# Attention values multiplied by half-height matmuls, and a ring of 20 slots: one change to an attention and ternary-FFN kernel

## The chip, the cores and the metric

The kernel runs on one NeuronCore of one Trainium2 chip. The metric is the device time of one execution in microseconds. TensorE is called PE here, its weight loads PEld, VectorE DVE, ScalarE ACT, GpSimd POOL, and SyncE's queue, which issues nearly all transfers, SP.

## What is computed

For each of 64 batches, x is 512 rows of 512, and the context 77 rows of 512:

```
q  = layernorm(x) @ Wq                    # 4 groups x 4 kv heads of 32; rope
k, v = ctx @ Wk, ctx @ Wv                 # 4 kv heads of 32; rope on k
score[h] = sum over groups g of q[g, h] @ k[h].T / sqrt(32)
x1 = x + mean over h of (softmax(score[h]) @ v[h]) @ Wo
xq = clip(round(layernorm(x1) / i_scale)) # i_scale = max |layernorm(x1)| / 127, over ALL batches
out = x1 + (xq @ ternary(W).T) * w_scale * i_scale + bias
```

Since the scores are summed over the groups, the kernel sums Wq over them beforehand and has 4 heads per row. Two things matter for this change: the product of the softmax with v, and that i_scale needs all of x1 before the first FFN product, so that the kernel has two stages.

## The kernel before

**Prologue.** The context is projected to keys and values, which are written to two scratch tensors in HBM (k_scr, v_scr), and the weights are prepared.

**Stage A** (steps 0 to 127 and a tail; `steps`, L295) works on half a batch per step: two tiles of 128 rows of x, called t = 0, 1. It is a software pipeline of eight stages (L81: PROJ, ROPE, SCORE, VALUE, HEAD, RESID, STAT, RSTD); step i does PROJ for half-batch i, ROPE for i-1, SCORE for i-2, VALUE for i-3 and so on. Each engine has its own instruction stream, in the order written; semaphores join them. PE's order in a step (L1183 to L1276): transposes of the rotated q (qr_sb) and of the head sums (os_sb), 16 transposes of x, 10 transposes of the exponentials (e_sb), scores (L1239), output projection y (L1250), projection of x (L1258), values (L1273). Transposes, scores and y use 64 of the 128 rows of the PE array each (HALF = 64), in pairs: one instruction with rows 0 to 63, one with rows 64 to 127. The projection and the values use all 128 rows.

The keys of the two tiles stand side by side in e_sb: 2 x 4 heads x 77 = 616 columns, cut in five chunks of 128 (`STARTS`, L51). A chunk's 128 columns become the rows of pT_sb; the values of the same keys stand in v_blk, each head's 34 columns (32 values, their mean with Wo, a one for the sum of the exponentials) in its own place with zeros elsewhere, so that heads don't mix. A chunk touches three heads (the middle one two), and all five accumulate in one PSUM bank:

```
for c in (0, 2, 4, 1, 3):
    at0, n = FIRST_HEAD[c] * VC, HEADS_OF[c]
    last = pe.matmul(bank[6][:, at0:at0 + n * VC], pT_sb[:, c, :], v_blk[:, slot, c, 0:n, :]..., start=c == 0, stop=c == 3)
last.then_inc(pv_done, 1)
```

ACT then copies the bank out (L698), and has in the same step, in this order, the copies of the transposed q (L709), of the transposed head sums (L717) and of the transposed x (L725).

**SP's queue in stage A** (L439 to L462), per batch and strictly in order: both halves of x of batch b (each after `added_t` says that the slot of batch b-4 is free), the store of x1 of batch b-4 to the output tensor, 12 small loads of values of batch b-1 (`v_fetch`, after `pv_done`), 4 small loads of keys of batch b (`k_fetch`, after `sc_done`). The last 16 batches' x1 stay in SBUF (SLOTS = KEPT = 16, x1_sb); 48 are stored and come back later. x itself has a ring of four batches (x_sb), and in stage B its place serves other tiles.

**Stage B** (L1292 to L1339 on PE) takes the batches from the slots: ACT and DVE quantise, PE transposes (L1300) and multiplies in fp16 with half-height pairs (L1317), ACT adds the mean, DVE the product (L1052), SP writes the result (`result_out`) and brings the next stored x1 in (`x1_back`). The two row halves of the PE array never add to one bank at the same time: each product is made in two parts, with the banks changed between them, and the wait `ffn_half` (L1307) in between; the next transposes stand between the parts.

## Time and profile before

| what | value |
|---|---|
| median of 3 runs | 1137.72 us (1136.8 to 1142.96) |
| the profiled execution | 1138.31 us, of which the span is 1136.5 us |
| PE busy | 1075.1 us, 95% of the span |
| DVE busy | 1015.8 us, 89% |
| ACT busy | 963.0 us, 85% |
| POOL busy | 729.6 us, 64% |
| stage A, about | 115 to 815 us of the span |
| stage B, about | 820 to 1136.5 us of the span |

The profile is of one execution. Its own time stands beside its span; the difference of 1.8 us lies around the span. Busy shares of the whole span mix two stages with different limits, so each stage has to be read by itself. A PE matmul's recorded length runs to the end of its result, and matmuls overlap, so the pace of a group is read from its starts.

### The profile page before, as it was taken

The page shows a single profiled execution, that of the slowest core. Times are in us where ns is not written, and L with a number is a line of the kernel's source. Part 1 is how long each engine was busy: PE and PEld are TensorE (multiplying, and loading weights), DVE is VectorE, ACT ScalarE, POOL GpSimd, SP SyncE. Part 2 cuts the span into 40 slices and gives each one's busy share as a digit, 9 for nine tenths or more (in the row PEclk, how much of TensorE's full clock was granted, in tenths as well). Part 3 has the DMA queues.
Part 4 walks back from the last instruction along what each step waited for, and adds up shares of the span by engine and source line. Part 5 has one row for each costly group of instructions (what it writes and reads, how often), then busy time and mean ns, then how long its engine had stood idle before and what let it go on. Part 6 is the DMA issues. An engine that isn't in the chain of part 4 may idle for free.

```text
span 1136.5 us, 44893 instructions
## 1 busy us (share of the span) xinstructions
PE 1075.1 (95%) x14007; PEld 865.5 (76%) x14007; DVE 1015.8 (89%) x1836; ACT 963.0 (85%) x2147; POOL 729.6 (64%) x1547
## 2 busy tenths in 40 slices
PE   7998999999999999999999999999599999999991
PEld 6997988988989988998889998998455555555540
DVE  4653898999999999999999999999789999999981
ACT  4564888988989889988899989999599999999980
POOL 4675998999999999999999999999500000000000
PEclk9999999999999999999999999999599999999996
DMA  8765366666676666766667653432049999999996
GB/s 290 228 176 162 85 205 189 211 189 214 177 223 183 210 216 187 221 194 198 207 195 222 184 154 106 121 104 67 1 180 408 421 424 426 426 407 371 411 395 267
DMA packets 119897, 262.97 MB, mean 231 GB/s; under 512 B 65193, under 2 KB 76649, under 8 KB 99378
## 3 DMA queue, kind: packets, MB, share of 16 engines
q1 hardware_dynamic: 119810, 262.44, 68.2%
q8 instruction: 17, 0.28, 0.1%
q14 instruction: 22, 0.18, 0.0%
q10 hardware_dynamic: 48, 0.07, 0.0%
HBM read 139.79 MB, written 122.64 MB: 231 GB/s over the span
## 4 chain that ended last, share of the span: by engine, by line
POOL 34%; issue 24%; PE 12%; ACT 9%; DMA 8%; DVE 6%; SPq 3%; POOLq 1%; ACTq 1%; DVEq 0%
POOL qa_sb L559 6%; POOL pw_sb L589 6%; POOL qr_sb L599 5%; ACT x_sb L789 5%; PE y_ps L1113 5%; DMA out_y<-x_sb 5%; POOL pw_sb L605 4%; POOL os_sb L619 3%; POOL o_sb L610 3%; DVE x_sb L1052 3%; ACT x_sb L772 2%; DMA x_sb<-out_y 2%; POOL ve_sb L576 2%; SPq L378 2%; POOL rs_sb L583 2%
## 5 line engine op out<-in xcount | busy, mean ns | idle before, releaser
L1258 PEld LDWEIGHTS xT_ps<-wqs,xT_sb 128*128 128x128 f32 x2048 | 239.2, 192 | 48.3 <-ACT xT_sb L725 48.3
L1258 PE MATMUL xT_ps<-wqs,xT_sb 128*128 128x128 f32 x2048 | 263.6, 282 | 2.8 <-ACT xT_sb L725 2.8
L978 DVE SCALAR_TENSOR_TENSOR x_sb<-x_sb,mv_sb,y_ps 128x512 f32 (+1 forms) x256 | 177.9, 736 | 3.2 <-PE y_ps L1250 3.2
L789 ACT ACTIVATE x_sb<-x_sb,mean 128x512 f32 (+1 forms) x256 | 168.7, 707 | 0.0
L1273 PE MATMUL pT_ps<-v_blk,pT_sb 128*128 128x102 f32 (+1 forms) x1280 | 163.6, 275 | 0.0
L689 ACT ACTIVATE sq_sb<-x_sb 128x512 bf16 (+1 forms) x256 | 160.8, 628 | 1.0 <-DVE x_sb L978 0.8
L1273 PEld LDWEIGHTS pT_ps<-v_blk,pT_sb 128*128 128x128 f32 x1280 | 155.2, 194 | 1.7 <-ACT pT_sb L738 1.0
L985 DVE TENSOR_REDUCE amax<-x_sb (+1 forms) x128 | 155.1, 1213 | 0.0
L748 ACT ACTIVATE e_sb<-e_sb,rs_sb 128x308 f32<-128x308 f32 x256 | 127.3, 544 | 16.2 <-DVE e_sb L961 6.6
L725 ACT ACTIVATE xT_sb<-xT_ps 128x1024 f32<-128x1024 f32 x128 | 131.3, 1026 | 3.0 <-PE xT_ps L1180 2.9
L1317 PE MATMUL sc_ps<-wT,x_sb 64*128 64x512 f16 x1024 | 133.5, 380 | 0.1
L583 POOL TENSOR_TENSOR rs_sb<-ve_sb,mhalf 128x4 f32 (+2 forms) x133 | 132.3, 995 | 0.5
L948 DVE TENSOR_REDUCE mx_sb<-sc_ps 128x8 f32<-128x616 f32 x128 | 102.4, 800 | 33.4 <-PE sc_ps L1239 28.8
L1317 PE MATMUL pT_ps<-wT,x_sb 64*128 64x512 f16 x1024 | 132.1, 377 | 0.1
L559 POOL TENSOR_TENSOR qa_sb<-q_sb,qcos 128x256 f32<-128x256 f32 x128 | 93.8, 733 | 28.4 <-ACT q_sb L756 22.2
L1239 PE MATMUL sc_ps<-k_blk,qT_sb 64*128 64x154 f32 x1024 | 101.5, 315 | 0.4 <-ACT oT_sb L717 0.3
L961 DVE TENSOR_TENSOR e_sb<-sc_ps,mx_sb 128x616 f32<-128x616 f32 x128 | 98.2, 767 | 0.0
L1250 PE MATMUL y_ps<-wst,oT_sb 64*128 64x512 f32 x512 | 96.9, 449 | 0.9 <-ACT oT_sb L717 0.9
L1052 DVE SCALAR_TENSOR_TENSOR x_sb<-sc_ps,cols,x_sb 128x512 f32 (+1 forms) x128 | 90.2, 747 | 7.8 <-PE sc_ps L1317 2.3
L698 ACT ACTIVATE pv_sb<-pT_ps 128x272 f32<-128x272 f32 x128 | 50.9, 398 | 53.2 <-PE pT_ps L1273 53.2
L772 ACT ACTIVATE x_sb<-x_sb,rs_sb 128x512 f32 (+1 forms) x128 | 85.4, 714 | 12.5 <-DMA x_sb<-out_y 5.6
L599 POOL TENSOR_TENSOR qr_sb<-qa_sb,qb_sb 128x256 f32<-128x256 f32 x128 | 93.7, 732 | 0.1
(140 smaller groups left out, 2286.0 us busy)
## 6 DMA issues: line engine op xcount, KB each, us to landing
out_y<-x_sb SPq DMA_DIRECT2D x112, 1024.0 KB, 10.2
x_sb<-in_x SPq DMA_DIRECT2D x128, 512.0 KB, 5.1
x_sb<-out_y SPq DMA_DIRECT2D x48, 1024.0 KB, 15.3
x_sb<-in_ctx SPq DMA_DIRECT2D x38, 256.0 KB, 4.5
k_blk<-k_scr SPq DMA_DIRECT2D x256, 9.6 KB, 1.7
v_blk<-v_scr SPq DMA_DIRECT2D x256, 10.2 KB
v_scr<-x_sb SPq DMA_DIRECT2D x38, 68.0 KB, 3.1
k_scr<-x_sb SPq DMA_DIRECT2D x38, 64.0 KB, 3.4
```

The lines of the kernel that those rows point to most:

```text
L559: pool.tensor_tensor(dst[:, :].rearrange("p (t h d) -> p t h d", t=2, h=HEADS), q_sb[:, :].rearrange("p (t h d) -> p t h d", t=2, h=HEADS) ...
L583: pool.tensor_tensor(rs_sb[:, bass.ds(js, 1), :, at].rearrange("p a t n -> p (a t) n"), ve_sb[:, k % 2, :, at], mhalf[:, :, at], ALU.pow). ...
L599: pool.tensor_tensor(qr_sb[:, kj % 2, :].rearrange("p (a b) -> p a b", b=2), qa_sb[:, :].rearrange("p (a b) -> p a b", b=2), swapped(qb_sb ...
L689: act.activation(sq_sb[:, :], x1_at(kj, gj, t), ACT.Square, scale=E ** -0.5, accum_out=mv_sb[:, (kj + BACK) % UN, t, 2:3]).then_inc(sq_don ...
L725: act.activation(xT_sb[:, :, :, :].rearrange("p t c (h r) -> p (t c) h r", h=2), rows_of(xT_ps, 0, 2 * EC), ACT.Copy).then_inc(xT_copied, 1)
L748: act.activation(e_sb[:, kj % 2, t, :], e_sb[:, kj % 2, t, :], ACT.Exp, scale=rs_sb[:, bass.ds(j, 1), t, 0]).then_inc(exp_done_t, 1)
L789: act.activation(u_sb[:, k % 2, t, :], x1_sb[:, bass.ds(x1_turn(g, k) + t * E, E)], ACT.Identity, bias=stat_of(mean1, j, t, back)).then_in ...
L978: dve.scalar_tensor_tensor(out=x1_at(kj, gj, t), in0=x_sb[:, kj // 2, 2 * (kj % 2) + t, :], scalar=mv_sb[:, kj, t, 0:1], in1=y_ps[:, t, :] ...
L985: dve.tensor_reduce(amax[:, bass.ds(2 * j, 2)], x1_at(kj, gj).rearrange("p (t e) -> p t e", t=2), AX.X, ALU.max, apply_absolute_value=True ...
L1258: last = pe.matmul(bank[0][:, t * HD:(t + 1) * HD], xT_sb[:, t, c, :], wqs[:, c, :], start=c == 0, stop=c == EC - 1)
L1273: last = pe.matmul(bank[6][:, at0:at0 + n * VC], pT_sb[:, c, :], v_blk[:, slot, c, 0:n, :].rearrange("p h d -> p (h d)"), start=c == 0, st ...
L1317: last = pe.matmul(bank[4 + t][:, :], q16T_sb[rows, 4 * par + t, c, :], wT[rows, c, :], start=False, stop=second == 1 and c == EC - 1)
```

## The change

1. **Values in halves.** The five chunks start at other columns (0, 128, 244, 372, 488), so that the middle one splits between the two tiles. Each chunk is multiplied in two halves of 64 rows. Tile t's output goes to bank 6 + t, four heads of 34 columns each, in the order of `COLUMN`. A half touches one or two heads (`keys_of`): ten matmuls with 34 or 68 columns in place of five with 102 or 68. Rows 0 to 63 and 64 to 127 never add to one bank at the same time: six matmuls go first (rows 0 to 63 to bank 6, rows 64 to 127 to bank 7), then PE waits for two of its own (`pv_half`), then four with the banks changed. v_blk has two places per chunk instead of three; the number of value loads stays 12. ACT's copy reads two banks, and has the same size.
2. **SP's order in stage A.** The first half of x for batch b+1 is now requested among the value loads of batch b-1: after 8 of the 12, before the last 4 and the key loads of batch b.
3. **Slots.** x_sb becomes the last four of 20 slots of one buffer (SLOTS = KEPT + XS). The tiles of stage B that lay in x_sb now lie over small tiles of stage A. When the last four batches have been added, SP reads the first four stored batches into these slots, before the first result is due; 44 reads are left for the time after it, in place of 48. The loop bounds of stage B follow (`FULL`).

The core of the diff:

```
@@ -47,9 +47,16 @@
 HALF = P // 2
 CHUNKS = 5
-STARTS = [min(c * P, 2 * SC - P) for c in range(CHUNKS)]
-FIRST_HEAD, HEADS_OF = (0, 1, 3, 4, 5), (3, 3, 2, 3, 3)
+STARTS = (0, P, SC - HALF, SC + HALF, 2 * SC - P)
+COLUMN = (0, 2, 1, 3)
+HALVES = {(0, 0): (0, 0), (0, 1): (0, 64), (1, 0): (0, 128), (1, 1): (0, 192), (2, 0): (0, 256),
+          (2, 1): (1, 0), (3, 0): (1, 64), (3, 1): (1, 128), (4, 0): (1, 192), (4, 1): (1, 244)}
+FIRST_VALUES, MORE_VALUES = ((0, 2), (1, 3), (2, 4)), ((3, 0), (4, 1))
 CROWS = B * CTX
 CT = CROWS // P
...
@@ -59,9 +66,12 @@
 UN = 2 * XS
 GRP = NP_ // UN
-SLOTS = 16
-KEPT = SLOTS
+KEPT = 16
+KEPT_TURNS = KEPT // XS
+SLOTS = KEPT + XS
 RING = SLOTS // XS
+assert (B - KEPT) % KEPT == 0
 ZEROED = 8
...
@@ -88,15 +98,27 @@
 ROPE_BASE = 10000.0
+def keys_of(c, n):
+    t, lo = HALVES[c, n]
+    hi = STARTS[c] + (n + 1) * HALF - t * SC
+    return t, lo, hi, range(lo // CTX, (hi - 1) // CTX + 1)
 def segments():
     out = []
     for c, start in enumerate(STARTS):
-        for n in range(2 * HEADS):
-            lo, hi = max(c * P, CTX * n), min(c * P + P, CTX * (n + 1))
-            if lo < hi:
-                assert FIRST_HEAD[c] <= n < FIRST_HEAD[c] + HEADS_OF[c]
-                out.append((c, lo - start, hi - lo, n - FIRST_HEAD[c], n % HEADS, lo - CTX * n))
+        rows = {}
+        for n in range(2):
+            t, lo, hi, heads = keys_of(c, n)
+            assert len(heads) <= 2
+            for h in heads:
+                a, b = max(lo, CTX * h), min(hi, CTX * (h + 1))
+                if (t, h) in rows and rows[t, h][1] == a:
+                    a = rows[t, h][0]
+                rows[t, h] = (a, b)
+        out += [(c, t * SC + a - start, b - a, h % 2, h, a - CTX * h) for (t, h), (a, b) in rows.items()]
     return out
...
@@ -124,13 +146,19 @@
         v_scr = nc.dram_tensor("v_scr", (CROWS, HEADS, VC), F32, kind="Internal").ap()
-        x_sb = sb("x_sb", [P, XS, TPB, E])
         with nc.sbuf_tensor("wkv_parts", [P, 2, EC, WC], F32R) as wkv_r, \
                 nc.sbuf_tensor("cT_parts", [P, 2, 2, EC, P], F32R) as cT_parts:
             pass
         PARTS = 2 * EC * WC + 2 * 2 * EC * P
         x1_sb = sb("x1_sb", [P, SLOTS * TPB * E])
+        x_sb = x1_sb[:, KEPT * TPB * E:].rearrange("p (k t e) -> p k t e", k=XS, t=TPB)
+        with nc.sbuf_tensor("qm_sb", [P, 2, 2, E], F32) as qm_sb, \
+                nc.sbuf_tensor("q16T_sb", [P, 2 * TPB, EC, P], F16) as q16T_sb, \
+                nc.sbuf_tensor("u_sb", [P, 2, TPB, E], F32) as u_sb, \
+                nc.sbuf_tensor("st_a", [P, NT], F32) as st_sb:
+            pass
+        st_a = st_sb[:, :]
         xT_sb = sb("xT_sb", [P, 2, EC, P])
         q_sb = sb("q_sb", [P, 2 * HD])
         qa_sb = sb("qa_sb", [P, 2 * HD])
...
@@ -216,13 +244,8 @@
         fpos = early(EC, E)
         fsum4 = early(EC)
         w16 = early(EC, E // 2).bitcast(F16)
-        assert at[0] <= SLOTS * TPB * E
-        qm_sb = x_sb[:, 3, :, :].rearrange("p (a b) e -> p a b e", a=2)
-        q16T_sb = x_sb[:, 0, :, :].bitcast(F16).rearrange("p a (t c r) -> p (a t) c r", t=2, c=EC)
-        u_sb = x_sb[:, 1:3, :, :]
-        st_a = x_sb[:, 2, 0, 0:NT]
+        assert at[0] <= KEPT * TPB * E
         xT_ps, y_ps, sc_ps, pT_ps = (
             stack.enter_context(nc.psum_tensor(n, [P, 2, 512], F32)) for n in ("xT_ps", "y_ps", "sc_ps", "pT_ps"))
...
@@ -434,35 +457,40 @@
                 sp.wait_ge(v_out[n], 16 * ((CT - n) // ORING + 1))
             for k in range(XS):
-                sp.sem_inc(x1_out[k], 16 * RING)
+                sp.sem_inc(x1_out[k], 16 * KEPT_TURNS)
+            def x_half(b, k, n):
+                at_least(sp, added_t, 4 * (b - XS) + 2 * n + 2)
+                sp.dma_start(x_sb[:, k, 2 * n:2 * n + 2, :].rearrange("p t e -> p (t e)"),
+                             xv[bass.ds(b, 1), :, 2 * n:2 * n + 2, :].rearrange("b p t e -> p (b t e)"))\
+                  .then_inc(x_in[2 * k + n], 16)
             def batch_step(b, k, g, store=True):
-                for n in range(2):
-                    at_least(sp, added_t, 4 * (b - XS) + 2 * n + 2)
-                    sp.dma_start(x_sb[:, k, 2 * n:2 * n + 2, :].rearrange("p t e -> p (t e)"),
-                                 xv[bass.ds(b, 1), :, 2 * n:2 * n + 2, :].rearrange("b p t e -> p (b t e)"))\
-                      .then_inc(x_in[2 * k + n], 16)
+                x_half(b, k, 1)
                 if store:
                     store_x1(b - XS, k, g - 1)
+                v_fetch(b - 1, k - 1, SEGS[:8])
+                if not isinstance(b, int) or b + 1 < B:
+                    x_half(b + 1, (k + 1) % XS, 0)
+                v_step(b - 1, k - 1, SEGS[8:])
+                k_fetch(b, k)
             def store_x1(b, k, g):
                 sp.dma_start(ov[bass.ds(b, 1)].rearrange("b p t e -> p (b t e)"),
-                             x1_sb[:, bass.ds((g % RING) * (XS * TPB * E) + k * TPB * E, TPB * E)])\
+                             x1_sb[:, bass.ds((g % KEPT_TURNS) * (XS * TPB * E) + k * TPB * E, TPB * E)])\
                   .then_inc(x1_out[k], 16)
             k_fetch(2, 2)
             v_fetch(2, 2)
             k_fetch(3, 3)
+            x_half(XS, 0, 0)
             with sp.Fori(1, (B - KEPT) // XS + 1) as g:
                 for k in range(XS):
                     batch_step(g * XS + k, k, g)
-                    v_fetch(g * XS + k - 1, k - 1)
-                    k_fetch(g * XS + k, k)
             for b in range(B - KEPT + XS, B):
                 batch_step(b, b % XS, b // XS, store=False)
-                v_fetch(b - 1, b - 1)
-                k_fetch(b, b)
             v_fetch(B - 1, B - 1)
             def result_out(g, k, b):
...
@@ -475,32 +503,39 @@
                 sp.wait_ge(y_out[k], (g - RING) * 16 + 16)
                 sp.dma_start(x1_sb[:, bass.ds(x1_turn(g, k), TPB * E)],
-                             ov[bass.ds(g * XS + k - SLOTS, 1)].rearrange("b p t e -> p (b t e)"))\
+                             ov[bass.ds(g * XS + k - KEPT, 1)].rearrange("b p t e -> p (b t e)"))\
                   .then_inc(x1_in[k], 16)
             for k in range(XS):
-                sp.wait_ge(x1_out[k], 16 * RING + 16 * ((B - KEPT) // XS))
+                sp.wait_ge(x1_out[k], 16 * KEPT_TURNS + 16 * ((B - KEPT) // XS))
             def two_out(g, k, first):
                 for n in range(2):
-                    result_out(g, k + n, (g * XS + k + n) - SLOTS + (B if first else 0))
+                    result_out(g, k + n, (g * XS + k + n) - KEPT + (B if first else 0))
             def two_back(j, n):
                 for m in range(2):
                     x1_back(j + (n + m) // XS, (n + m) % XS)
-            for j in range(0, SLOTS, 2):
+            for k in range(XS):
+                sp.wait_ge(added_t, 4 * (B - XS + k) + 4)
+                sp.dma_start(x1_sb[:, (KEPT + k) * TPB * E:(KEPT + k + 1) * TPB * E],
+                             ov[k].rearrange("p t e -> p (t e)")).then_inc(x1_in[k], 16)
+            for j in range(0, KEPT, 2):
                 two_out(j // XS, j % XS, True)
                 n = j - 2 + SLOTS
                 if j >= 2:
                     two_back(n // XS, n % XS)
-            with sp.Fori(RING, (B - SLOTS) // XS) as g:
+            FULL = (B - SLOTS + 2) // XS
+            with sp.Fori(KEPT_TURNS, FULL) as g:
                 for k in range(0, XS, 2):
                     two_out(g, k, False)
                     two_back(g + (k - 2) // XS + RING, (k - 2) % XS)
-            for j in range(B - SLOTS, B, 2):
+            for j in range(FULL * XS, B, 2):
                 two_out(j // XS, j % XS, False)
                 n = j - 2 + SLOTS
                 if n < B:
...
@@ -695,8 +730,8 @@
                     act.wait_ge(pv_done, j + 1)
                     at_least(act, o_part, 2 * j)
-                    act.activation(pv_sb[:, :, :, :].rearrange("p t h d -> p (t h d)"),
-                                   bank[6][:, 0:2 * HEADS * VC], ACT.Copy).then_inc(pv_copied, 1)
+                    act.activation(pv_sb[:, :, :, :].rearrange("p t h d -> p t (h d)"),
+                                   pT_ps[:, :, 0:HEADS * VC], ACT.Copy).then_inc(pv_copied, 1)
                 if score:
                     j, kj, gj = score
...
@@ -1180,6 +1215,16 @@
                     last = pe.transpose(ps[0:src.shape[1], n, at0:at0 + HALF], src[lo:hi, :], ident[lo:hi, lo:hi])
                 return last
+            def values(c, half, slot, start, stop):
+                t, _, _, heads = keys_of(c, half)
+                rows = slice(half * HALF, (half + 1) * HALF)
+                places = sorted(h % 2 for h in heads)
+                cols = sorted(COLUMN[h] for h in heads)
+                out_at = bank[6 + t][:, 0:HEADS * VC].rearrange("p (h d) -> p h d", d=VC)
+                return pe.matmul(out_at[:, cols[0]:cols[-1] + 1:max(cols[-1] - cols[0], 1), :], pT_sb[rows, c, :],
+                                 v_blk[rows, slot, c, places[0]:places[-1] + 1, :], start=start, stop=stop)
             def step(i, k, g):
                 proj, rope, score, value, head, resid, stat, rstd = (stage(i, k, g, lag) for lag in range(RSTD + 1))
                 if proj:
...
@@ -1266,13 +1311,14 @@
                         pe.wait_ge(v_in[slot], gj * (2 * V_DMAS * 16) + (kj // 4 + 1) * (V_DMAS * 16))
                     pe.wait_ge(pT_copied, j + 1)
-                    for c in (0, 2, 4, 1, 3):
-                        at0, n = FIRST_HEAD[c] * VC, HEADS_OF[c]
-                        last = pe.matmul(bank[6][:, at0:at0 + n * VC], pT_sb[:, c, :],
-                                         v_blk[:, slot, c, 0:n, :].rearrange("p h d -> p (h d)"),
-                                         start=c == 0, stop=c == 3)
+                    for n, (half, c) in enumerate([(half, cs[half]) for cs in FIRST_VALUES for half in range(2)]):
+                        last = values(c, half, slot, start=n < 2, stop=False)
+                        if n >= 4:
+                            last.then_inc(pv_half, 1)
+                    pe.wait_ge(pv_half, 2 * j + 2)
+                    for n, (half, c) in enumerate([(half, cs[half]) for cs in MORE_VALUES for half in range(2)]):
+                        last = values(c, half, slot, start=False, stop=n >= 2)
                     last.then_inc(pv_done, 1)
             steps(pe, step)
...
```

PE, stage A, the values and the start of the next step (qr_sb is the rotated q). Before:

```order
L1258 MATMUL xT_ps<-wqs,xT_sb 128x128 x7
L1273 MATMUL pT_ps<-v_blk,pT_sb 128x102 [waits pT_copied,v_in0]
L1273 MATMUL pT_ps<-v_blk,pT_sb 128x68
L1273 MATMUL pT_ps<-v_blk,pT_sb 128x102 x3
L1180 MATMUL sc_ps<-ident,qr_sb 128x64 [waits qr_ready,sub_done,x_in4]
```

and with the change:

```order
L1303 MATMUL xT_ps<-wqs,xT_sb 128x128 x7
L1225 MATMUL pT_ps<-v_blk,pT_sb 128x34 [waits pT_copied,v_in0]
L1225 MATMUL pT_ps<-v_blk,pT_sb 128x34
L1225 MATMUL pT_ps<-v_blk,pT_sb 128x68 x2
L1225 MATMUL pT_ps<-v_blk,pT_sb 128x34 x2
L1225 MATMUL pT_ps<-v_blk,pT_sb 128x2x34 [waits pv_half]
L1225 MATMUL pT_ps<-v_blk,pT_sb 128x2x34 x3
L1215 MATMUL sc_ps<-ident,qr_sb 128x64 [waits qr_ready,sub_done,x_in7]
```

Ten matmuls stand where five stood, with one wait of PE for itself after the sixth; nothing else stands between them.

SP, stage A, around the value loads of one batch. Before:

```order
L443 DMA x_sb<-in_x 128x1024
L450 ISA
L450 DMA out_y<-x_sb 128x2048
L378 ISA [waits pv_done]
L378 DMA v_blk<-v_scr 77x34
...
L378 DMA v_blk<-v_scr 77x34
L293 ISA
L372 ISA [waits sc_done]
L372 DMA k_blk<-k_scr 32x77
```

and with the change:

```order
L401 DMA v_blk<-v_scr 13x34
L316 ISA
L465 ISA [waits added_t]
L465 DMA x_sb<-in_x 128x1024
L401 DMA v_blk<-v_scr 77x34
L401 DMA v_blk<-v_scr 38x34
L401 ISA
L401 DMA v_blk<-v_scr 39x34
L401 DMA v_blk<-v_scr 77x34
L316 ISA
L395 ISA [waits sc_done]
```

A load of x (in_x) with its own wait now stands between the eighth and the ninth value load, ahead of the key loads.

## Rows read from the trace of the kernel before

**Rows 1.** The page, part 1: engines, busy us and share, instructions.

```profile
PE 1075.1 (95%) x14007; PEld 865.5 (76%) x14007; DVE 1015.8 (89%) x1836; ACT 963.0 (85%) x2147; POOL 729.6 (64%) x1547
```

**Rows 2.** Windows: stretch and length in us, busy us by engine, PEclk, DMA share, GB/s.

```profile
200.00:400.00 200.00, 196.88 (x2553) 178.66 (x2548) 194.57 (x366) 179.42 (x438) 189.88 (x399) 1.00 0.66 201
800.00:820.00 20.00, 12.35 (x67) 8.15 (x63) 14.70 (x22) 10.68 (x31) 11.09 (x29) 0.53 0.00 1
880.00:920.00 40.00, 40.00 (x618) 20.68 (x616) 39.10 (x65) 39.51 (x64) 0.00 (x0) 1.00 1.01 422
1130.00:1137.00 7.00, 0.00 (x0) 0.00 (x0) 0.00 (x0) 0.00 (x0) 0.00 (x0) 0.50 0.05 21
```

**Rows 3.** The copy of the transposed exponentials, one per step, two stretches.

```profile
L738 ACT ACTIVATE pT_sb<-pT_ps x15: 692/695/714, 699.5 to 775.1; 128x640 f32<-128x640 f32 x15
...
L738 ACT ACTIVATE pT_sb<-pT_ps x125: 692/695/715, 121.7 to 800.9; 128x640 f32<-128x640 f32 x125
```

**Rows 4.** Waits, 130 to 800 us: total us, times, longest.

```profile
ACT pv_sb L698 <- PE pT_ps L1273: 49.7, 122, 0.5
PEld xT_ps L1258 <- ACT xT_sb L725: 43.8, 121, 0.4
...
PE sc_ps L1180 <- DMA x_sb<-in_x: 8.3, 12, 1.4
```

**Rows 5.** Timeline of ACT, one step: start, length from first to last, group.

```profile
506.19 0.40 ACT L698 ACTIVATE pv_sb<-pT_ps 128x272 f32<-128x272 f32 x1 [0.46 <-PE pT_ps L1273]
...
506.94 1.02 ACT L725 ACTIVATE xT_sb<-xT_ps 128x1024 f32<-128x1024 f32 x1
```

**Rows 6.** Timeline of PEld, the same step.

```profile
506.18 0.58 PEld L1180 LDWEIGHTS xT_ps<-ident,x_sb 64*128 64x128 f32 x16
...
507.09 0.56 PEld L1239 LDWEIGHTS sc_ps<-k_blk,qT_sb 64*128 64x128 f32 x8
...
508.28 1.86 PEld L1258 LDWEIGHTS xT_ps<-wqs,xT_sb 128*128 128x128 f32 x16 [0.37 <-ACT xT_sb L725]
510.06 1.20 PEld L1273 LDWEIGHTS pT_ps<-v_blk,pT_sb 128*128 128x128 f32 x10
511.36 0.14 PEld L1180 LDWEIGHTS sc_ps<-ident,qr_sb 64*128 64x128 f32 x2
```

**Rows 7.** Timeline of PE, the same step.

```profile
507.62 0.74 PE L1250 MATMUL y_ps<-wst,oT_sb 64*128 64x512 f32 x4
...
510.17 1.26 PE L1273 MATMUL pT_ps<-v_blk,pT_sb 128*128 128x102 f32 x10
```

**Rows 8.** Groups by form, 400 to 600 us: busy us, mean ns of one.

```profile
L1273 PEld LDWEIGHTS pT_ps<-v_blk,pT_sb 128*128 128x128 f32 x370 | 44.3, 192 | 0.0
...
L1180 PEld LDWEIGHTS xT_ps<-ident,x_sb 64*128 64x128 f32 x584 | 21.4, 139 | 0.0
L1239 PEld LDWEIGHTS sc_ps<-k_blk,qT_sb 64*128 64x128 f32 x288 | 20.7, 186 | 0.9
```

**Rows 9.** Timelines of PE (two rows) and PEld (one), stage B.

```profile
1065.13 1.03 PE L1317 MATMUL sc_ps<-wT,x_sb 64*128 64x512 f16 x8
...
1107.95 2.16 PE L1317 MATMUL sc_ps<-wT,x_sb 64*128 64x512 f16 x16
...
1109.06 0.55 PEld L1317 LDWEIGHTS sc_ps<-wT,x_sb 64*128 64x128 f16 x8 [0.58 <-PE sc_ps L1317]
```

**Rows 10.** Timeline of SP's queue, stage A.

```profile
388.29 6.54 SPq L378 DMA_DIRECT2D v_blk<-v_scr  x12
395.12 1.82 SPq L372 DMA_DIRECT2D k_blk<-k_scr  x4
397.61 0.95 SPq L443 DMA_DIRECT2D x_sb<-in_x  x2
```

**Rows 11.** The page, part 6: transfers, KB each, us to landing.

```profile
out_y<-x_sb SPq DMA_DIRECT2D x112, 1024.0 KB, 10.2
...
x_sb<-out_y SPq DMA_DIRECT2D x48, 1024.0 KB, 15.3
```

More of the change, by code:

```diff
@@ L149, in build @@
         k_blk = sb("k_blk", [P, 2, SC])
-        v_blk = sb("v_blk", [P, 2, CHUNKS, max(HEADS_OF), VC])
+        v_blk = sb("v_blk", [P, 2, CHUNKS, 2, VC])
+        qcos = sb("qcos", [P, TPB, D])
+        qsin = sb("qsin", [P, TPB, D])
+        wqs = sb("wqs", [P, EC, HD])
+        wst = sb("wst", [P, 2, E], F32R)
         bn_sb = sb("bn_sb", [P, 2, 2, 6])
@@ L272, in build @@
             sem(n) for n in ("sc_done", "mx_ready", "sub_done", "exp_done_t"))
-        pT_done, pT_copied, pv_done, pv_copied = (
-            sem(n) for n in ("pT_done", "pT_copied", "pv_done", "pv_copied"))
+        pT_done, pT_copied, pv_half, pv_done, pv_copied = (
+            sem(n) for n in ("pT_done", "pT_copied", "pv_half", "pv_done", "pv_copied"))
         rinv_ready, o_part, o_ready, os_ready, wq_mean, wq_centred = (
@@ L795, in turn @@
                 left = B - j if isinstance(j, int) else B
-                mean_back = not isinstance(j, int) or j + 1 >= SLOTS
+                mean_back = not isinstance(j, int) or j + 1 >= KEPT
                 if left > 2:
@@ L809, in _ @@
             add_mean(0, 0, range(TPB), False)
-            for j in range(SLOTS):
-                turn(j // XS, j % XS, j + 2 >= SLOTS)
-            with act.Fori(RING, B // XS - 1) as g:
+            for j in range(KEPT):
+                turn(j // XS, j % XS, j + 2 >= KEPT)
+            with act.Fori(KEPT_TURNS, B // XS - 1) as g:
                 for k in range(XS):
@@ L1081, in _ @@
             quantise(0, 1, False)
-            for j in range(SLOTS):
-                turn(j // XS, j % XS, j + 2 >= SLOTS)
-            with dve.Fori(RING, B // XS - 1) as g:
+            for j in range(KEPT):
+                turn(j // XS, j % XS, j + 2 >= KEPT)
+            with dve.Fori(KEPT_TURNS, B // XS - 1) as g:
                 for k in range(XS):
```

20 lines of the change are left out of this document (8 added, 12 removed).

## The prediction

> **What bounds the kernel now.** I read the page's busy shares first: PE 95%, DVE 89%, ACT 85% [rows 1]. They mix two stages, so the windows come next [rows 2]. In stage A (200 to 400 us) PE is busy 196.9 of 200 us, DVE 194.6, POOL 189.9, ACT 179.4, the granted clock is 1.00 (the 2.4 GHz level), and the transfers have room, 0.66. In stage B (880 to 920 us) the 16 DMA engines are full, 1.01 at 422 GB/s, beside a full PE. A step of stage A takes 75.6 us / 14 = 5.40 us where nothing disturbs it, and 679.2 / 124 = 5.48 us on the whole [rows 3]. The difference, 9.6 us over the stage, is nearly all in one wait: PE for a load of x, 12 times, 8.3 us [rows 4].
>
> Is it PE that sets 5.40 us? Two waits recur in each step [rows 4]: ACT for the values (0.4 us, 122 times), and PE's weight loads "for ACT's copy of x" (0.37 us, 121 times). The second is not ACT's. In one step ACT's copy ends at 506.94 + 1.02 = 507.96 [rows 5], the projection's first weight load starts at 508.28 [rows 6], and y, with 64 array rows, ends at 507.62 + 0.74 = 508.36 [rows 7]. PE is going from half-height to full-height work there and empties first. The first wait shows that ACT is held by PE. So stage A is PE's own sequence, with ACT's copies hung on the end of the values: whatever PE adds between the projection and the end of the values lengthens the step.
>
> **The change, part by part.**
>
> *Values.* First their pace. The ten weight loads of the five matmuls (fp32 is two passes) stretch over 1.20 us, the last recorded as 0.19: (1.20 - 0.19) / 9 = 0.112 us from load to load, the same for 102 and 68 columns [rows 6]. The projection, 128 columns, has (1.86 - 0.19) / 15 = 0.111. So weight loads set this pace, not columns, and narrower products gain nothing. A half needs its own load. Ten halves are twenty loads, in ten pairs that run side by side, as the scores do: 8 loads, 4 pairs, (0.56 - 0.19) / 3 = 0.123 us a pair with 154 columns [rows 6]. What does a pair cost with at most 68 columns? Lower bound: the transposes' (0.58 - 0.14) / 7 = 0.063 us [rows 6], also 64 rows of fp32. Upper bound: 0.123. The records of single loads decide: full-height value loads 192 ns, half-height loads of the scores 186, of the transposes 139 [rows 8]. A half-height load of an ordinary fp32 product thus takes as long as a full one, and I take 0.112 for the pair. Columns at the scores' rate are 0.123 / 154 = 0.8 ns each: 0.08 us for 102, 0.055 for 68, 0.03 for 34.
>
> The change of height: after the last value load, at 510.06 + 1.20 - 0.19 = 511.07, the first load of the half-height transposes starts at 511.36 [rows 6], 0.29 us later where 0.112 would do, and no wait is noted. That is 0.18 us. It now stands before the values, since the projection stays full-height, and what was behind them goes. What was behind them doesn't pay back: the next work behind the values that counts is ACT's copy of them (0.12 us after their end, 0.40 long) and the transposes into the same banks that wait for it; both hang on the end of the values, as before.
>
> PE's wait for itself: in the last batch of stage B the two parts of a product stand directly behind each other with the same kind of wait. A group of 8 there takes 1.03 us, which is (1.03 - 0.38) / 3 = 0.217 from pair to pair; 16 without a stop would be 7 x 0.217 + 0.38 = 1.90, and are 2.16 [rows 9]. The stop costs 0.26 us from the end of the columns to the next start, and the load engine idles 0.58. Here the next load (0.107) comes on top, since it can't be made ahead of the wait.
>
> The sum, first load to end of the last columns. Before: 9 x 0.112 + 0.107 + 0.08 = 1.20 us. After: 0.18 (height) + 8 x 0.112 + (0.107 + 0.03 + 0.26) (the stop) + 0.107 + 0.055 = 1.64 us. **That is 0.44 us more per step, 128 times: +56 us.** Bounds: with no change of height to pay before the values, 0.26, +33 us; with the stop at the whole 0.58 of idle that [rows 9] notes, 0.18 + 0.58 - 0.1 = 0.66, +84 us. I take 56, since both prices are read at the same kind of boundary.
>
> On the stop, the Trainium skill (TensorE: Matmul & The Clock Gate, Single matmul latency) gives (398 + N) / 2.4 ns for one warm bf16 matmul. For N = 34 that is 0.18 us in place of my 0.29, an estimate, and the sum would be 14 us lower by it. The row has the semaphore's way back in it, the formula has not, so the row's is used.
>
> *SP's order.* Per batch SP issues 12 value loads in 6.54 us, 4 key loads in 1.82, then both halves of x together [rows 10], well after the slot is free; the late x loads are the 8.3 us. The first half of x now goes ahead of four value loads and the key loads, some 6.54 / 3 + 1.82 = 4.0 us earlier, against a longest wait of 1.4 us. Steps that last 0.44 us longer give another 0.9 us a batch. **-8 us**; bounds 0 and -9.6. What is now queued behind that x load's wait, four value loads and the keys, is due more than a step later, and SP has 11.7 us per batch for about 10 us of issuing. ACT's copy from two banks has the same size: nothing.
>
> *Slots.* In stage B the engines run at 422 GB/s until the results are out, and a read is 1024 KB, 1.05 MB [rows 2, 11]. Four of 48 reads go to where the DMA idles (800 to 820 us, 1 GB/s [rows 2]): 4 x 1.05 / 0.422 = **-10 us**. Bounds: 0, should the end hang on the last results alone; -13, the 10 us and the stalls of stage B's engines for late reads beyond it. The tail after 1130 us, where one engine in sixteen is busy (0.05) [rows 2], stays.
>
> Sum against the profiled execution, which lies 0.6 us above the median: 1138 + 56 - 8 - 10 = **1176 us**.
>
> **The rivals.**
>
> *Half-height loads at the transposes' pace.* If a 64-row load costs 0.063 us a pair, the values take 0.18 + 8 x 0.063 + (0.063 + 0.03 + 0.26) + 0.063 + 0.055 = 1.16 us, 0.04 less than now, and nothing is left of the 56: 1138 - 5 - 8 - 10 = 1115 us, faster. The whole change stops being slower below a pair's pace of about 0.08 us. For it: the transposes are half-height fp32 and reach it. Against it: 186 ns beside 139 in [rows 8].
> The Trainium skill (TensorEngine Tiling (Array Packing), Theoretical Speedup) promises up to 2x where a dimension is at most 64, which speaks for this rival; the scores' pace of 0.123 does not bear it out.
>
> *The stops overlap.* If emptying for the height and for the wait cost only some 0.15 us per step together, because the array empties for both at once, or ACT's chain behind the values has more slack than I read: 1138 + 19 - 18 = 1139 us, no change.
>
> *PE's instruction queue loses its lead.* Before, PE's sequencer has taken the next step's waits while the values still run; now it stands at `pv_half`, and the four or five waits of the next step come after it. If that adds the 0.2 us of two of them: 1176 + 26 = 1202 us.
>
> *The ring does nothing*, if stage B's end hangs on PE: 1186 us, inside my range.
>
> **How the numbers follow.** Forecast, with the ring's rival, 0.74; fast loads 0.12; overlap 0.06; lost lead 0.08. Measurements here tell 0.5%, 5.7 us, from no change. Faster: the fast loads and a sliver of the overlap, 0.13. Same: most of the overlap, 0.05. Slower: 0.82. The range leaves out the fast loads and half of the two small cases: 1148 (the low bound 1138 + 33 - 9.6 - 13 = 1148) to 1202.
>
> **What would show it.** In the changed profile: steps of 5.8 to 5.9 us (5.40 now); in the timeline of PE's loads, values of about 1.6 us in two groups, six halves and four, with 0.4 us between their loads, paces of 0.11 and not 0.06 inside them, and an idle of PE's loads put down to PE's own values; DVE and POOL under 92% in stage A; no waits for x; 44 reads in stage B and its end some 10 us nearer to its begin. A value part under 1.2 us would refute the main term, and an unchanged length of stage B the third.

## The result, and the profile after

The changed kernel takes **1179.16 us** (median of 4 runs, 1177.36 to 1180.27), beside 1137.84 before. The ratio is 1.037, with a 95% interval of 1.033 to 1.040. The prediction said 1176, slower, with a range of 1148 to 1202. So direction and size came out. Of the three terms of its sum, the values' step and the ring came out, and the third, SP's order, had the wrong sign; the total is near in part by luck. The experiments are mostly about that third term.

The profiled execution took 1180.27 us, its span is 1178.5. Part 1 of its page, to compare with [rows 1]:

```profile
PE 1115.4 (95%) x15287; PEld 884.6 (75%) x15287; DVE 1017.0 (86%) x1836; ACT 953.6 (81%) x2147; POOL 728.0 (62%) x1547
```

PE has 1280 matmuls more, ten for each of 128 steps, and 40.3 us more busy time. Its share is still 95%. The windows, columns as in [rows 2]:

```profile
200.00:400.00 200.00, 192.77 (x2687) 170.08 (x2688) 180.37 (x337) 162.11 (x403) 174.03 (x371) 1.00 0.60 185
930.00:970.00 40.00, 40.00 (x618) 20.63 (x614) 39.05 (x64) 39.58 (x64) 0.00 (x0) 1.00 1.01 416
```

In stage A, DVE and POOL fell to 90 and 87% of the time, and PE is idle more than before, not less (7.2 us of 200 beside 3.1). Stage B is as it was: full transfers, full PE. The steps show in the copy of the transposed exponentials; the first row is the undisturbed end of the stage, the second is all of it:

```profile
L773 ACT ACTIVATE pT_sb<-pT_ps x16: 715/724/727, 752.2 to 839.8; 128x640 f32<-128x640 f32 x16
...
L773 ACT ACTIVATE pT_sb<-pT_ps x128: 697/724/737, 111.1 to 860.1; 128x640 f32<-128x640 f32 x128
```

An undisturbed step takes 87.6 / 15 = 5.84 us (before: 5.40, [rows 3]). From here on stage A is this row's first to last start: 749.0 us, where the kernel before has 694.2 (its copies start from 111.6 to 805.8). Stage B with the tail is the rest of the span: 1178.5 - 860.1 = 318.4 us, before 1136.5 - 805.8 = 330.7. So **stage A gained 54.8 us and stage B lost 12.3**.

The values in the timeline of PE's weight loads, first a step inside the loop, then one at its turn (start, length from first to last, group, idle before it). They answer to [rows 6]:

```profile
794.96 0.75 PEld L1225 LDWEIGHTS pT_ps<-v_blk,pT_sb 64*128 64x128 f32 x12
795.92 0.52 PEld L1225 LDWEIGHTS pT_ps<-v_blk,pT_sb 64*128 64x128 f32 x8 [0.21 <-PE pT_ps L1225]
796.31 0.26 PEld L1215 LDWEIGHTS sc_ps<-ident,qr_sb 64*128 64x128 f32 x4
...
800.69 0.75 PEld L1225 LDWEIGHTS pT_ps<-v_blk,pT_sb 64*128 64x128 f32 x12
801.64 0.52 PEld L1225 LDWEIGHTS pT_ps<-v_blk,pT_sb 64*128 64x128 f32 x8 [0.21 <-PE pT_ps L1225]
802.40 0.23 PEld L1215 LDWEIGHTS sc_ps<-ident,qr_sb 64*128 64x128 f32 x4 [0.23 <-issue]
```

Two groups, six halves and four. The pairs of loads in the first follow each other by (0.75 - 0.19) / 5 = 0.112 us. The stop between the groups is put down to PE's own values. Behind the values the half-height transposes start 0.39 us after the second group's start, without a gap; at the loop's turn it is 0.76, with an idle of 0.23 that nothing but the issue ends. The columns and the forms, in PE's timeline and in the groups of 400 to 600 us:

```profile
498.62 1.62 PE L1225 MATMUL pT_ps<-v_blk,pT_sb 64*128 64x34 f32 x20
```

```profile
L1225 PEld LDWEIGHTS pT_ps<-v_blk,pT_sb 64*128 64x128 f32 x660 | 41.9, 187 | 14.4 <-PE pT_ps L1225 6.8 <-DMA v_blk<-v_scr 4.9
```

1.62 us for the values where [rows 7] has 1.26, and a half-height load is recorded with 187 ns where a full one had 192 [rows 8]. The waits of 130 to 850 us (engine, what waits, for whom: total us, times, longest) answer to [rows 4]:

```profile
ACT pv_sb L733 <- PE pT_ps L1225: 119.1, 122, 1.8
POOL qa_sb L594 <- ACT q_sb L791: 72.9, 122, 1.7
DVE mx_sb L983 <- PE sc_ps L1284: 63.9, 121, 1.0
...
PEld pT_ps L1225 <- PE pT_ps L1225: 25.1, 122, 0.2
PEld pT_ps L1225 <- DMA v_blk<-v_scr: 15.5, 31, 1.0
PE pT_ps L1225 <- DMA v_blk<-v_scr: 9.0, 23, 0.8
```

No load of x is waited for any more. But the **values** now are, 23 times by PE and 31 times by its weight loads; the same list of the kernel before has no such wait. SP's queue in the same stretch, to compare with [rows 10]:

```profile
505.46 0.39 SPq L481 DMA_DIRECT2D out_y<-x_sb  x1
506.03 5.77 SPq L401 DMA_DIRECT2D v_blk<-v_scr  x8
512.09 0.38 SPq L465 DMA_DIRECT2D x_sb<-in_x  x1
512.57 1.55 SPq L401 DMA_DIRECT2D v_blk<-v_scr  x4
514.41 1.82 SPq L395 DMA_DIRECT2D k_blk<-k_scr  x4
516.93 0.38 SPq L465 DMA_DIRECT2D x_sb<-in_x  x1
517.66 0.39 SPq L481 DMA_DIRECT2D out_y<-x_sb  x1
```

SP hardly pauses: a batch's 19 transfers are issued from end to end, over 12.2 us here.

### The profile page after: what moved, and what is told of

Read it like the earlier page. It is cut to its first block, busy times and chain, and to the rows that moved or that the text cites. A ratio compares the mean times of both kernels' runs of the same rounds, so it can differ in the third digit from the quotient of the medians.

```text
span 1178.5 us, 47445 instructions
## 1 busy us (share of the span) xinstructions
PE 1115.4 (95%) x15287; PEld 884.6 (75%) x15287; DVE 1017.0 (86%) x1836; ACT 953.6 (81%) x2147; POOL 728.0 (62%) x1547
## 4 chain that ended last, share of the span: by engine, by line
PE 51%; SPq 32%; issue 9%; DVE 3%; DMA 2%; ACT 1%; POOL 1%; DVEq 0%; ACTq 0%; POOLq 0%
SPq L401 22%; PE sc_ps L1363 10%; PE pT_ps L1363 10%; PE xT_ps L1303 6%; PE pT_ps L1225 6%; PE y_ps L1148 5%; SPq L395 5%; SPq L465 3%; PE sc_ps L1284 2%; PE xT_ps L1215 2%; DMA v_blk<-v_scr 2%; SPq L481 2%; PE y_ps L1295 2%; PE pT_ps L1215 2%; PE xT_ps L1137 1%
## 5 line engine op out<-in xcount | busy, mean ns | idle before, releaser
L1225 PE MATMUL pT_ps<-v_blk,pT_sb 64*128 64x68 f32 (+1 forms) x2560 | 197.3, 282 | 21.6 <-DMA v_blk<-v_scr 9.0
L1225 PEld LDWEIGHTS pT_ps<-v_blk,pT_sb 64*128 64x128 f32 x2560 | 164.9, 189 | 54.4 <-PE pT_ps L1225 26.4
L824 ACT ACTIVATE u_sb<-x_sb,mean 128x512 f32 (+1 forms) x256 | 168.6, 707 | 0.0
L724 ACT ACTIVATE sq_sb<-x_sb 128x512 bf16 (+1 forms) x256 | 167.1, 653 | 1.0 <-DVE x_sb L1013 0.8
L1363 PE MATMUL sc_ps<-wT,q16T_sb 64*128 64x512 f16 x1024 | 133.3, 380 | 0.1
L1363 PE MATMUL pT_ps<-wT,q16T_sb 64*128 64x512 f16 x1024 | 132.1, 377 | 0.1
L1087 DVE SCALAR_TENSOR_TENSOR x_sb<-sc_ps,cols,u_sb 128x512 f32 (+1 forms) x128 | 90.2, 746 | 7.3 <-PE sc_ps L1363 1.5
L594 POOL TENSOR_TENSOR qb_sb<-q_sb,qsin 128x256 f32<-128x256 f32 x128 | 94.0, 734 | 0.0
```

Of the source, the lines that this page charges most:

```text
L594: pool.tensor_tensor(dst[:, :].rearrange("p (t h d) -> p t h d", t=2, h=HEADS), q_sb[:, :].rearrange("p (t h d) -> p t h d", t=2, h=HEADS) ...
L724: act.activation(sq_sb[:, :], x1_at(kj, gj, t), ACT.Square, scale=E ** -0.5, accum_out=mv_sb[:, (kj + BACK) % UN, t, 2:3]).then_inc(sq_don ...
L824: act.activation(u_sb[:, k % 2, t, :], x1_sb[:, bass.ds(x1_turn(g, k) + t * E, E)], ACT.Identity, bias=stat_of(mean1, j, t, back)).then_in ...
L1225: return pe.matmul(out_at[:, cols[0]:cols[-1] + 1:max(cols[-1] - cols[0], 1), :], pT_sb[rows, c, :], v_blk[rows, slot, c, places[0]:places ...
L1363: last = pe.matmul(bank[4 + t][:, :], q16T_sb[rows, 4 * par + t, c, :], wT[rows, c, :], start=False, stop=second == 1 and c == EC - 1)
```

## The experiments

Twelve kernels ran, in three groups of four: e1 to e4, e5 to e8, and e9, e10, e11 and e13. The kernel before, run beside each group, took 1134.4, 1134.5 and 1134.8 us; ratios are against those. The changed kernel was measured once, beside 1137.84, so a difference between it and an experiment is uncertain by some 3 us. The lengths of stages A and B are each of one profiled execution.

**e1_values: the values alone.** Part 1 of the change, put into the kernel before: `STARTS`, `HALVES`, the two groups with `pv_half`, ACT's copy from two banks. SP's order and the 16 slots stay.

> The kernel before with the halved values alone (SP's old order, 16 slots). Theory (PE pays a change of height and a stop, 0.44 us a step): undisturbed steps 5.83 us in place of 5.40, +54 to +56 us, of which 5 to 8 come back because longer steps make the loads of x less late: 1184 to 1190 us. Rival (SP's queue, 32% of the chain that ended last in the changed kernel, sets the longer step through its new order): undisturbed steps stay near 5.4 us and the time is under 1150 us.

Measured: 1179.44 us, ratio 1.039 (1.035 to 1.043); stage A 740.2 us, B 327.7. That is 45.0 us more than before, so the values carry the whole loss. The rest of the change gives back nothing in sum. The rival fell. The theory's step of 5.83 us came, but its 1184 to 1190 us was missed by 5; it was reckoned from 1138 us and not from 1134.4.

**e3_ring: the slots alone.** Part 3 of the change without the other two: full-height values, SP's old order.

> The kernel before with the ring of 20 slots alone. Theory (four reads fewer in a stage B that the DMA sets): stage A as before with its 8 us of late x, stage B 10 to 13 us shorter, 1125 to 1128 us. Rival (the end of stage B hangs on PE, and the 12 us gained there come from elsewhere): 1135 to 1138 us.

Measured: 1127.82 us, ratio 0.993 (0.990 to 0.996); stage A 693.2, B 320.7. In the traces the ring takes 10.0 us off stage B and leaves A alone. By the medians the gain is 6.6 us (4.5 to 10.9).

**e2_full: the change without the halves.** Full-height values, ring, SP's new order.

> The changed kernel with the full-height values back: new order of SP and ring of 20 alone. Theory: steps 5.40 us, 1138 - 12 (stage B) - 8 (no late x) = 1118 us; if value loads are late as in the changed kernel (11 us there) up to 1130 us. Rival (SP's order lengthens the step): steps of 5.7 us or more, over 1155 us.

Measured: 1147.59 us, ratio 1.011 (1.007 to 1.015), between the theory's upper end and the rival; both missed. It differs from e3_ring by SP's order alone and is 19.8 us slower. Its waits, 130 to 790 us:

```profile
PEld pT_ps L1291 <- DMA v_blk<-v_scr: 26.3, 41, 1.4
PE pT_ps L1291 <- DMA v_blk<-v_scr: 18.0, 33, 1.2
```

In e3_ring loads of x are waited for, 6.6 us in ten waits. The new order turned that into waits for values, 18.0 us on PE and 26.3 on its weight loads, which overlap.

**e4_nostop: the change without PE's stop.** Each half adds to a place of its own, so nothing has to wait. The kernel leaves out the sum of the two places, so it computes something else; its loads, matmuls and copies are as many and as large.

```
-                out_at = bank[6 + t][:, 0:HEADS * VC]
+                out_at = bank[6 + half][:, t * HEADS * VC:(t + 1) * HEADS * VC]
...
-                        if n >= 4:
-                            last.then_inc(pv_half, 1)
...
-                    pe.wait_ge(pv_half, 2 * j + 2)
```

> The changed kernel without the stop: rows 0 to 63 always go to bank 6 and rows 64 to 127 always to bank 7, so nothing has to be waited for. It leaves out the sum of the two banks' parts: ACT copies the first tile's two parts, and the second tile's are dropped. Theory: the stop costs 0.29 us a step (0.26 and a load that can't be made ahead), the change of height stays: steps 5.55 us, 1179 - 36 = 1143 us. Rival (the halves' own loads or SP's queue make the step long): at most 10 us less, 1169 us or more.

Measured: 1171.62 us, ratio 1.030 (1.025 to 1.035). By the total the stop seems to cost only 7.5 us, as the rival had it, and the theory's 1143 us was missed. But an undisturbed step is 5.52 us, 0.32 less, as the theory had it, and that would be 40 us over the stage. The waits, 130 to 790 us, say where they went:

```profile
PEld pT_ps L1225 <- DMA v_blk<-v_scr: 37.7, 40, 2.4
PE pT_ps L1225 <- DMA v_blk<-v_scr: 29.9, 36, 2.2
```

PE is ready earlier and waits for the values instead. Something on the side of the loads has a pace of its own.

**e7_half_old: the change with SP's old order.**

```
+                x_half(b, k, 0)
                 x_half(b, k, 1)
...
-                v_fetch(b - 1, k - 1, SEGS[:8])
-                if not isinstance(b, int) or b + 1 < B:
-                    x_half(b + 1, (k + 1) % XS, 0)
-                v_step(b - 1, k - 1, SEGS[8:])
+                v_fetch(b - 1, k - 1)
```

> The change with SP's order of before: half-height values and the ring of 20 slots, both halves of x again issued after the store's predecessors and before the value loads. Theory (the values cost 0.44 us a step and the ring gives 10 us, while the new SP order costs instead of giving): 1179.4 of the values alone less 10 = 1169 us, 1165 to 1173, about 10 us under the whole change; SP's queue has pauses in every batch. Rival (the SP order gives the 8 us that were forecast): 1187 us, over the whole change's 1179.

Measured: 1170.6 us (1169.35 to 1171.54), ratio 1.032 (1.029 to 1.035). So the new order costs 8.6 us in the change by the medians, 6 by the ratios; the forecast had it give 8. The expected pause of SP's queue in every batch did not come: while batches are stored it pauses in fewer than half of them.

**e5_half_late and e6_full_late: the first half of x behind all twelve value loads**, once with the change's halves, once with full-height values.

```
-                v_fetch(b - 1, k - 1, SEGS[:8])
+                v_fetch(b - 1, k - 1)
                 if not isinstance(b, int) or b + 1 < B:
                     x_half(b + 1, (k + 1) % XS, 0)
-                v_step(b - 1, k - 1, SEGS[8:])
```

> The change with one DMA moved: the first half of the next x goes behind all twelve value loads and ahead of the key loads, instead of between the eighth and the ninth. Theory (splitting the run of value loads is what makes SP's queue too long for a batch): value loads are late less often, 1167 to 1172 us. Rival (what costs is the wait ahead of the x load, wherever it stands, since loads are queued behind it): 1176 us or more, and now it is the key loads that come late.

> Full-height values as in the kernel before, the ring of 20 slots, and the first half of the next x behind all twelve value loads. Two steps last only 10.8 us here, so SP's queue is the tighter. Theory (splitting the value loads is what costs): 1120 to 1128 us, no more than the 1128 of the ring alone. Rival (the wait ahead of the x load costs): 1135 to 1150 us, near the 1147.6 with the split run.

Measured: e5 1176.98 us (ratio 1.039, 1.035 to 1.042), e6 1146.38 us (ratio 1.010, 1.007 to 1.013). Splitting the value loads is not the cause: both theories fell by their numbers. But the rivals' mechanism fell too, for what is queued behind that wait is hardly ever late: key loads are waited for twice in e5 and once in e6 (0.7 and 0.5 us on PE). The waits of e6 are for x, as in the kernel before and more of them.

```profile
PEld sc_ps L1197 <- issue: 31.5, 43, 1.4
...
PE sc_ps L1197 <- DMA x_sb<-in_x: 25.5, 43, 1.2
```

Another load is late, and the time is that of e2_full within 1.3 us. That suggested a third theory: the queue as a whole is full.

**e8_nostop_old: no stop, SP's old order.** The edits of e4 and e7 together; like e4 it leaves out the sum of the two places.

> The change without PE's stop and with SP's order of before; the sum of the two banks' parts is left out, so each half writes a place of its own. With the new SP order the same edit gave back 0.32 us a step but lost most of it to late value loads. Theory: with SP's queue free of that, 128 x 0.32 = 41 us less than the half-height kernel with the old order, 1125 to 1135 us, and what is left over the ring alone (1128) is the change of height less the narrower pairs, 0.1 us a step. Rival (the stop costs under 0.1 us and something else in the half-height values is slow): 1155 us or more.

Measured: 1151.55 us (1145.78 to 1157.43), ratio 1.014 (1.008 to 1.020), between theory and rival. Undisturbed steps take 5.52 us here too; the mean is 5.73, with 23 waits for x (14.0 us). The old order is not free of the limit either.

### How much SP needs for a batch

The store of a finished batch is issued once per batch, so its rows give the mean length of a batch. Between 200 and 750 us, before, then after, then e2_full (count, shortest, median and longest issue in ns, first and last start):

```profile
L450 SPq DMA_DIRECT2D out_y<-x_sb x42: 356/357/357, 200.2 to 649.9; - x42
```

```profile
L481 SPq DMA_DIRECT2D out_y<-x_sb x42: 385/386/389, 208.1 to 696.4; - x42
```

```profile
L464 SPq DMA_DIRECT2D out_y<-x_sb x42: 380/380/381, 201.5 to 672.2; - x42
```

That is 449.7 / 41 = 10.97 us before, 488.3 / 41 = 11.91 after, 470.7 / 41 = 11.48 in e2. Against them stands what SP needs: the mean lengths of the 19 issues in the trace of each kernel, added up, and the gaps between them, taken as medians (0.09 to 0.4 us each, 3.65 to 3.68 in all).

| kernel | issues + gaps = SP's need | two undisturbed steps | batch measured |
|---|---|---|---|
| before | 7.24 + 3.67 = 10.91 | 10.80 | 10.97 |
| e1_values | 7.75 + 3.67 = 11.42 | 11.67 | 11.66 |
| e3_ring | 7.21 + 3.67 = 10.88 | 10.80 | 10.95 |
| e7_half_old | 7.75 + 3.67 = 11.42 | 11.67 | 11.64 |
| after | 8.15 + 3.68 = 11.83 | 11.67 | 11.91 |
| e5_half_late | 8.09 + 3.65 = 11.74 | 11.66 | 11.83 |
| e2_full | 7.73 + 3.68 = 11.41 | 10.80 | 11.48 |
| e6_full_late | 7.72 + 3.65 = 11.37 | 10.80 | 11.45 |
| e8_nostop_old | 7.73 + 3.67 = 11.40 | 11.03 | 11.48 |
| e4_nostop | 8.13 + 3.68 = 11.81 | 11.03 | 11.89 |

In every row the batch is the larger of the two, within 0.1 us. The kernel before is in it too: **SP's queue, not PE, set its pace through the middle of stage A.**

Where a queue never pauses, its issues and gaps must add up to the batch, so the table alone could agree by construction. That it never pauses is seen in the gaps of single batches, from 250 us on and as long as batches are stored. In the kernel before they add up to 3.51, 4.17, 3.53 and 3.63 us for the four batches of a turn of SP's loop, the same to 0.02 us in every turn; in the change to 3.67, 3.54, 4.28 and 3.55. A queue that waited for an engine would hardly repeat like that, and where PE has the longer turn it doesn't: in e7 the sum at one and the same place in the turn is between 3.51 and 4.42. The loop's turn is in these sums and not in the medians; with their means, 3.71 and 3.76, the need is 10.95 us before and 11.91 in the change, against 10.97 and 11.91 measured.

Two things lengthened the queue. The halves' list of value loads adds 0.5 us (the seventh and eighth load take 0.51 and 0.38 us in place of 0.26 and 0.23, the third 0.84 for 0.62). The new order adds 0.4 to 0.5 us, net nearly all in the value loads behind the store: the second and third are 1.0 us longer together, the fourth and fifth 0.7 shorter. The timeline of SP's queue shows it, first before (four value loads behind the store), then after (three):

```profile
519.00 2.73 SPq L378 DMA_DIRECT2D v_blk<-v_scr  x4
```

```profile
518.35 3.40 SPq L401 DMA_DIRECT2D v_blk<-v_scr  x3
```

The second and third load take 1.20 and 1.27 us on the mean in the changed kernel, and 0.62 and 0.79 in e7_half_old.

**The test: the store on another queue.** If the queue is full, taking one transfer off it must cure every variant, whatever its order. ACT's queue issues the store, where ACT has waited for `added_t` anyway:

```
+                    if kj % 2 and stored(j, gj):
+                        act.wait_ge(x1_out[kj // 2], 16 * KEPT_TURNS + gj * 16)
+                        act.dma_start(ov[bass.ds(gj * XS + kj // 2, 1)].rearrange("b p t e -> p (b t e)"),
+                                      x1_sb[:, bass.ds((gj % KEPT_TURNS) * (UN * 2 * E) + (kj - 1) * 2 * E, TPB * E)])\
+                           .then_inc(x1_out[kj // 2], 16)
...
-            def batch_step(b, k, g, store=True):
+            def batch_step(b, k, g, store=False):
```

ACT's loop is split in two, with one turn written out between them, since only the first 48 batches are stored. e9 is the change with this edit, e10 is e3_ring, e13 is e2_full, and e11 is e8_nostop_old, without the sum as before.

> The whole change, with one transfer moved: the 1024 KB store of a finished batch is issued from ACT's queue, behind a wait that ACT has anyway, and no longer from SP's. Theory (SP's queue is the bound where loads come late: in the change the issues of a batch take 8.15 us and the gaps between them 3.68, 11.83 in all, against 11.66 us for two undisturbed steps): without the store SP needs at most 11.2 us, and under 10 if its packets are what slows the value loads behind it; no value load is late, 1164 to 1170 us, a batch of 11.66 us. Rival (the order of the loads makes them late, whatever room SP has): 1175 us or more. Second rival (the issue on ACT stretches ACT's chain, which PE waits for): over 1175 us with no late loads.

> The ring of 20 slots with full-height values and SP's old order, the store on ACT's queue. SP needs 7.21 + 3.67 = 10.88 us a batch with the store, and two undisturbed steps last 10.80: by the theory SP is the bound already in the kernel before, and the late loads of x are its sign, not the order's. Theory: no waits for x, 5.40 us a step all through, 1128 - 9 = 1119 us, 1115 to 1122. Rival (x is late for its place in the order): 1128 us as the ring alone.

> Full-height values, ring of 20 slots, the new SP order with the first half of the next x between the value loads, the store on ACT's queue. The same with the store on SP's queue was 1147.6 us, SP needing 7.73 + 3.68 = 11.4 us a batch. Theory (SP's total is what counts, and the new order only made the loads behind the store slower to issue): 1115 to 1122 us, the same as with the old order. Rival (the order itself makes value loads late): 1135 us or more.

> Half-height values without PE's stop, SP's old order, the store on ACT's queue; the sum of the two banks' parts is left out, so each half writes a place of its own. With the store on SP's queue it was 1151.6 us and SP's batch 11.46 us against 11.03 for two undisturbed steps. Theory (SP's queue hid what the stop costs): steps of 5.52 us all through, 1170.6 - 127 x 0.316 = 1130 us, 1126 to 1136. Rival (the stop's removal leaves other waits in the step): 1145 us or more with a median step over 5.6 us.

Measured, all four inside the theory's range or 0.01 us from its edge:

| kernel | us (ratio, interval) | batch, measured | stage A / B, us |
|---|---|---|---|
| e9_half_store | 1168.18 (1.029, 1.027 to 1.031) | 11.65 | 735.7 / 317.7 |
| e10_full_store | 1117.16 (0.983, 0.981 to 0.985) | 10.79 | 686.2 / 323.4 |
| e13_full_new_store | 1114.99 (0.982, 0.980 to 0.983) | 10.79 | 684.5 / 319.3 |
| e11_nostop_store | 1133.03 (0.998, 0.997 to 1.000) | 11.01 | 700.5 / 320.1 |

The batch is two undisturbed steps everywhere. No load of values is late in any of them, and of x one in e10 and one in e11. SP's issues now add up to 6.9, 7.0, 6.6 and 7.1 us a batch (in the table's order) in place of 8.15, 7.21, 7.73 and 7.73. The edit changes one thing more: the store lands sooner from ACT's queue (4.2 us after its issue in e13, 6.5 in e2; 5.0 in e10, 8.0 in e3), and so do the loads of x in e10 (4.2 us, 5.7 in e3). So these four runs alone can't tell the time of SP's issues from the way the bytes take; the gaps that repeat to 0.02 us with the store on SP, and no longer without it, can. SP's timeline in e13_full_new_store has pauses now, 0.76 us ahead of the x load and 0.57 ahead of the next:

```profile
505.11 1.82 SPq L378 DMA_DIRECT2D k_blk<-k_scr  x4
507.69 0.37 SPq L448 DMA_DIRECT2D x_sb<-in_x  x1
508.25 4.27 SPq L384 DMA_DIRECT2D v_blk<-v_scr  x8
513.09 0.38 SPq L448 DMA_DIRECT2D x_sb<-in_x  x1
```

Its window of 200 to 400 us shows what a stage A looks like where PE has no pause, beside 196.88 in [rows 2]:

```profile
200.00:400.00 200.00, 199.98 (x2601) 181.53 (x2598) 197.96 (x371) 181.46 (x446) 192.65 (x409) 1.00 0.63 204
```

The issue costs ACT's sequencer 0.35 us, while ACT's own work goes on (timeline of ACT):

```profile
509.83 0.69 ACT L760 ACTIVATE pT_sb<-pT_ps 128x640 f32<-128x640 f32 x1
510.29 0.35 ACTq L767 DMA_DIRECT2D out_y<-x_sb  x1
510.41 0.63 ACT L711 ACTIVATE sq_sb<-x_sb 128x512 bf16 x1
```

The Trainium skill (DMA: Bandwidth & Descriptors, Issuing engines are not separate DMA queues) says that starting transfers from several engines saves only the sequencer's time, "which is usually small relative to the DMA itself". Here the engines' share was 0.60 to 0.66 before and after, so no bandwidth was lacking or won; that the store lands sooner from ACT's queue is not in that sentence. The second half did not hold here: the sequencer's time was the bound, and one transfer of nineteen taken off it made e2_full 32.6 us faster (1147.59 to 1114.99).

**e13_full_new_store is faster than both kernels**, by 1.8% against before. It has the change's ring and SP order, the store on ACT's queue, and no halves.

## Why the prediction was right, and where it was wrong

*The values (forecast +0.44 us a step, +56).* Right by the step, in its parts too; the 56 were 45 in the kernel. The pair's pace is 0.112, not 0.063. From the projection's last load to the first of the values are 0.31 us (0.20 over the pace; forecast 0.18). From the sixth half's loads to the next group are 0.39 (forecast 0.397). An undisturbed step grew by 0.43 to 0.44. The parts come from the runs without late loads:

- The stop: e9 less e11, 11.65 - 11.01 = 0.64 a batch, 0.32 a step. Forecast 0.29 (0.26 and the exposed load 0.107 with its columns, 0.03, less the 0.112 that an unstopped group takes there anyway). In seven steps of eight it is 0.28; at the loop's turn it is 0.58.
- The rest, change of height and narrower pairs: e11 less e10, (11.01 - 10.79) / 2 = 0.11. Forecast 0.15 (the same sum without the stop, 1.35, less 1.20).

Free of SP's limit, halves cost 1168.2 - 1115.0 = 53.2 us. In e1_values they cost 45.0, since longer steps also gave SP's queue its time back.

*SP's order (forecast -8).* **This is the step that failed, in sign.** Its last sentence had the queue with "11.7 us per batch for about 10 us of issuing". The 10 us are near the three groups of [rows 10] and the store added up: 6.54 + 1.82 + 0.95 + 0.36 = 9.7. The gaps between the groups, 0.29 and 0.67 us, stood in the same rows (388.29 + 6.54 ends 0.29 before 395.12, 395.12 + 1.82 ends 0.67 before 397.61) and were left out, and so was the growth of the issues themselves. The need was 10.91 before and 11.83 after, against 11.67 available. A queue with 1.7 us to spare can be reordered for nothing; this one had none. It cost 6 to 9 us in the change (e7 to after) and 19.8 with full-height values (e3 to e2). The reason given for the 8 us, that x would come in time, did come true; the price was paid by the values.

The same misreading stands in the prediction's first part. "Stage A is PE's own sequence" holds for the undisturbed step. The 8.3 us of late x were read as a matter of place in the order. They were the sign that SP's 10.91 us is over PE's 10.80; e10 shows it: with the old order and nothing but the store moved it has one wait for x, and is 10.7 us faster than e3_ring.

*The ring (forecast -10).* Right within the noise: stage B is 10.0 us shorter in e3, 12.3 after, 8.5 from e1 to e7, and the medians are 6.6 us (e3) and 8.8 (e1 to e7) lower.

*The sum.* 1134.5 (before) + 45.0 (values) - 8.8 (ring, e1 to e7) + 8.6 (order) = 1179.3. The sum closes by itself, since each step is the difference to the next kernel; it shows sizes and proves nothing. The forecast's total was near by luck in part: the order's error, some 17 us, was met by the values, which were 45 and not 56 on top of a queue-bound kernel, and by a kernel before that ran some 3 us lower beside the experiments.

*The rivals.* Half-height loads at the transposes' pace: refuted by 187 ns and 0.112 us. The stops overlap: refuted, 0.43 and not 0.15. The ring does nothing: refuted by e3. PE's queue loses its lead: its sign is there in one step of eight, at the loop's turn, where 0.23 us of idle follow the values and the stop costs 0.3 us more, 0.04 a step. The rival had priced it at 0.2 a step; it is 5 us and not 26. That it is the sequencer's lead is the likely reading; the trace has no row for the jump.

*The signs.* Steps of 5.84, 1.62 us of values in two groups, the idle put down to PE's own values, DVE and POOL under 92%, no waits for x, stage B shorter: all seen. That no load of x was waited for was listed as a sign of success. It was not one: the wait had moved to the values. A sign for a reordered queue should be the sum over all its loads.
